# Cross attention tile loop: one stretch of projections, the value products between the two rounds of scores, and more buffers

## The reference

```python
qh = (q @ Wq.T).reshape(B, Lq, H, D).transpose(0, 2, 1, 3)
kh = (k @ Wk.T).reshape(B, Lk, H, D).transpose(0, 2, 1, 3)
vh = (v @ Wv.T).reshape(B, Lk, H, D).transpose(0, 2, 1, 3)
qh = _layernorm(qh, gq, bq) * scale
kh = _layernorm(kh, gk, bk)
attn = jax.nn.sigmoid(jnp.einsum('bhqd,bhkd->bhqk', qh, kh))
x = jnp.einsum('bhqk,bhkd->bhqd', attn, vh)
x = x.transpose(0, 2, 1, 3).reshape(B, Lq, C)
return x @ Wp.T + bp
```

## Time and profile before

| What | Value |
|---|---|
| Time, median of 3 runs | 3021.32 us (3021.06 to 3024.84) |
| The profiled execution's own time | 3023.51 us |
| Its span in the profile | 3021.8 us |
| Mean granted TensorE clock | 0.990 |
| PE busy | 2954.1 us, 98% of the span |
| ACT, DVE, POOL busy | 1474.4, 1409.8 and 873.7 us |

### The profile page before, as it was taken

How to read it: one execution, slowest core, us unless ns; L and a number is a source line. 1 busy time by engine, 2 the same in 40 slices (tenths; PEclk the granted TensorE clock), 3 DMA queues, 4 the chain that set the end, 5 groups by cost and what they waited for, 6 DMA issues and landing times.

```text
span 3021.8 us, 69076 instructions
## 1 busy us (share of the span) xinstructions
PE 2954.1 (98%) x28514; PEld 2327.0 (77%) x28514; DVE 1409.8 (47%) x1962; ACT 1474.4 (49%) x1450; POOL 873.7 (29%) x615
## 2 busy tenths in 40 slices
PE   6999999999999999999999999986999999999999
PEld 4777777777777777777777777753999998999998
DVE  5333333333333333333333333336658856657754
ACT  1444444444444444444444444440646555646554
POOL 3444444444444444444444444430000000000000
PEclk8999999999999999999999999997999999999999
DMA  5000000000000000000000010001455555555553
GB/s 202 28 24 28 24 28 24 28 24 28 24 28 24 28 24 28 24 28 24 28 24 28 24 28 24 28 1 56 154 181 182 183 194 195 195 183 190 178 188 133
DMA packets 53359, 231.64 MB, mean 77 GB/s; under 512 B 6056, under 2 KB 6312, under 8 KB 31920
## 3 DMA queue, kind: packets, MB, share of 16 engines
q1 hardware_dynamic: 53296, 230.74, 22.5%
HBM read 230.19 MB, written 0.52 MB: 76 GB/s over the span
## 4 chain that ended last, share of the span: by engine, by line
PE 95%; DVE 3%; issue 1%; ACT 1%; DMA 0%; POOL 0%; POOLq 0%; SPq 0%; DVEq 0%; ACTq 0%
PE kv_ps L1041 38%; PE f_ps L1288 22%; PE o_ps L1087 12%; PE s_ps L1075 12%; PE y_ps L1272 5%; PE kv_ps L1062 3%; PE pm L1155 1%; DVE w_lo L632 1%; DVE pre L909 0%; ACT w_hi L522 0%; PE pm L1203 0%; DMA wk_rows<-wk_dram 0%; PE kv_ps L1034 0%; PE pm L1144 0%; DVE lin_norm L809 0%
## 5 line engine op out<-in xcount | busy, mean ns | idle before, releaser
L483 ACT ACTIVATE probs<-s_ps 128x2048 f32<-128x2048 f32 x392 | 737.7, 1882 | 718.6 <-PE s_ps L1075 718.5
L429 POOL TENSOR_TENSOR k_var<-k_var,neg_half 128x16 f32<-128x16 f32 x196 | 571.0, 2913 | 15.5 <-POOL k_var L425 0.2
L419 POOL TENSOR_TENSOR ctx_lo<-ctx_raw,ctx_hi 128x512 fp32r<-128x512 f32 x196 | 251.8, 1285 | 1117.9 <-DVE ctx_hi L673 1117.9
L698 DVE TENSOR_TENSOR k_n<-k_centred,k_var 128x496 f32<-128x496 f32 x196 | 134.4, 686 | 711.4 <-POOL k_var L429 711.4
L632 DVE TENSOR_TENSOR w_lo<-w_raw,w_hi 128x2048 fp32r<-128x2048 f32 x160 | 366.4, 2291 | 175.4 <-ACT w_hi L522 175.3
L1288 PE MATMUL f_ps<-h_hi,w_hi 128*128 128x256 f32 x1536 | 428.8, 279 | 0.0
L1288 PE MATMUL f_ps<-h_lo,w_hi 128*128 128x256 f32 x1536 | 427.8, 279 | 0.0
L1288 PE MATMUL f_ps<-h_hi,w_lo 128*128 128x256 f32 x1536 | 427.8, 279 | 0.0
L1087 PE MATMUL o_ps<-probs,v_sb 128*32 128x256 f32 x6272 | 380.8, 383 | 0.2 <-ACT probs L483 0.2
L1041 PE MATMUL kv_ps<-wk_hi,ctx_hi 128*128 128x512 f32 x784 | 347.3, 443 | 4.3 <-DVE q_lo L751 2.8
L522 ACT ACTIVATE w_hi<-w_raw 128x2048 fp32r<-128x2048 f32 x160 | 305.9, 1913 | 70.2 <-PE y_ps L1272 62.4
(11 more groups left out here) (194 smaller groups left out, 4850.7 us busy)
## 6 DMA issues: line engine op xcount, KB each, us to landing
w_raw<-w_dram SPq DMA_DIRECT2D x160, 1024.0 KB, 4.8
ctx_raw<-ctx_dram SPq DMA_DIRECT2D x196, 256.0 KB, 2.6
qkv_w<-qkv_w_dram SPq DMA_DIRECT2D x1, 3072.0 KB, 13.1
bias_rows<-bias_rows_dram SPq DMA_DIRECT2D x1, 1280.0 KB, 16.6
wq<-wq_dram SPq DMA_DIRECT2D x1, 1024.0 KB, 5.5
wk_rows<-wk_dram SPq DMA_DIRECT2D x1, 1024.0 KB, 7.5
wv<-wv_dram SPq DMA_DIRECT2D x1, 1024.0 KB, 9.7
out_w<-out_w_dram SPq DMA_DIRECT2D x1, 1024.0 KB, 17.7
```

Of the source, the lines that this page charges most:

```text
L419: g.tensor_tensor(ctx_lo[r % 2][:], raw[r % 4][:], ctx_hi[r % 2][:].bitcast(f32), ALU.subtract).then_inc(ctx_lo_made, 1)
L429: g.tensor_tensor(k_var[:, 2], k_var[:, 1], neg_half[:].to_broadcast([P, H]), ALU.pow)\
L483: s.activation(probs[half][:], s_ps[:], ACT.Sigmoid).then_inc(probs_made, 1)
L698: v.tensor_tensor(k_n[:, :, 0:D - 1], k_c[:, :, 0:D - 1], per_row(k_var[:, 2], D - 1), ALU.mult)\
```

## The change

There are four buffers `v_sb` instead of two, and three `probs` instead of two: round 0 takes `probs[0]` and `probs[1]` by turns, round 1 always `probs[2]`. On PE a step now has the transposes of tile r-1 first, then all 24 projection matmuls of tile r, round 0 of tile r-1, the value products of tile r-2, and round 1 of tile r-1. On DVE the values of tile r are copied in step r, ahead of `normalise`, no longer in step r+1. ACT's round 0 no longer waits for the value products that stand ahead of it. Nothing after the attention is changed.

```diff
-        v_sb = [sb(f"v_sb{i}", [P, C], f32, attn) for i in range(2)]
-        probs = [sb(f"probs{i}", [P, HG, 2, TOK], f32, attn) for i in range(2)]
+        v_sb = [sb(f"v_sb{i}", [P, C], f32, attn) for i in range(4)]
+        probs = [sb(f"probs{i}", [P, HG, 2, TOK], f32, attn) for i in range(3)]
...
+        def probs_of(r, half):
+
+            return probs[2] if half else probs[r % 2]
...
                 act.wait_ge(s_made, n_of(it, r, 2, half + 1))
-                act.wait_ge(av_made, n_of(it, r, 2, half + 1))
-                s.activation(probs[half][:], s_ps[:], ACT.Sigmoid).then_inc(probs_made, 1)
+                wait(act, av_made, n_of(it, r, 2, 2 if half else -1))
+                s.activation(probs_of(r, half)[:], s_ps[:], ACT.Sigmoid).then_inc(probs_made, 1)
...
                 dve.wait_ge(v_made, n_of(it, r, 1, 1))
-                wait(dve, av_made, n_of(it, r, 2))
-                v.tensor_copy(v_sb[r % 2][:], kv_ps[:, 1]).then_inc(v_copied, 1)
+                wait(dve, av_made, n_of(it, r, 2, -4))
+                v.tensor_copy(v_sb[r % 4][:], kv_ps[:, 1]).then_inc(v_copied, 1)
...
-                copy_values(it, r - 1)
                 split_turned(it, r - 1)
                 if more:
                     high_part(it, r + 1)
                 if keys:
                     sum_squares(it, r)
+                    copy_values(it, r)
                     normalise(it, r)
...
+            copy_values(0, 0)
             normalise(0, 0)
...
-                if project_it:
-                    projection(it, r, 0, 6)
                 turn_keys(it, r - 1)
                 if project_it:
-                    projection(it, r, 6, 12)
+                    projection(it, r, 0, 24)
+                scores(it, r - 1, 0)
                 if not too_early(it, r - 2):
                     attend(it, r - 2, 0)
                     attend(it, r - 2, 1)
-                scores(it, r - 1, 0)
-                if project_it:
-                    projection(it, r, 12, 24)
                 scores(it, r - 1, 1)
```

More of the change, by code:

```diff
@@ L1086, in attend @@
                         first = P * grp + D * h
-                        ins = t.matmul(o_ps[D * h:D * h + D, grp], v_sb[r % 2][:, first:first + D],
-                                       probs[half][:, h, j], start=False, stop=False, skip_group_check=True)
+                        ins = t.matmul(o_ps[D * h:D * h + D, grp], v_sb[r % 4][:, first:first + D],
+                                       probs_of(r, half)[:, h, j], start=False, stop=False, skip_group_check=True)
                 ins.then_inc(av_made, 1)
             def step(it, r, project_it=True):
-                if project_it:
-                    projection(it, r, 0, 6)
                 turn_keys(it, r - 1)
                 if project_it:
-                    projection(it, r, 6, 12)
+                    projection(it, r, 0, 24)
+                scores(it, r - 1, 0)
                 if not too_early(it, r - 2):
```

## The result

The changed kernel takes 3001.15 us in the median of 4 runs (2998.84 to 3003.03); the kernel before takes 3023.03 us beside it (3021.06 to 3024.84). The ratio is 0.9927, 95% interval 0.991 to 0.9945: faster by 0.7%, 22 us. The profiled execution took 3001.42 us, its span is 2999.7 us, 22.1 less than before.

The account below looks back on a forecast made before the run. PE's back-to-back instructions were taken to bound the tile loop. The step would go from 10.07 to 10.05 us: 194 steps x -0.02 = -4, plus 1.5 one-time, gives -2.5 and 3019 us, range 3004 to 3032.

Parts of the forecast that it names:

- What bounds the kernel: Tile loop: PE never waits, so a step lasts as long as PE's instructions one behind the other, 10.07 us.
- Projections as one run of 24: PE's projections in a step: three runs (6, 6, 12) become one that settles to closer spacing, 5.34 us.
- The second rival: Second half of the 24 projections: the run does not settle, 0.07 us more per step, 3032 us; chance 0.10.
- Round 1 to transposes: PE from round 1 of scores to the transposes: 0.91 us, plus 0.06 between bounds of nothing and 0.10.
- Between the rounds: PE from round 0 to round 1: the sigmoid's 2.35 us outlasts the products' 2.11, a new wait of about 0.24.
- ACT's wait in one step of four: Sigmoid of round 0: its wait on a register instruction costs 0.08 to 0.09 us there, 0.02 per step.
- DVE's order: Values copied ahead of `normalise` on DVE: costs nothing, with 0.8 us left before the transposes would wait.
- The third rival: Transposes wait because DVE's copy stretches POOL's power: +114 us, 3135 us; chance 0.03.
- One-time: Outside the repeated steps: 2.6 us more at the start, 1.1 back at the end, together 1.5 more.
- Only the change-overs count: PE's step: fewer changes of matmul form, no wait for the sigmoid; step 9.81 us, total 2972 us; chance 0.05.
- The fourth rival: PE's clock falls because of a short idle piece in each step: +190 us if one step in ten, 3210; chance 0.02.
- The mechanism's own range: Forecast's wait of 0.24 us eating the saved change-over, chance 0.75: 2997 to 3036 us, mostly 3007 to 3028.

Follow-up runs that it names:

- e8: Changed kernel with PE's order of before, keeping only buffers, ACT's relaxed waits and DVE's earlier copy: 3027.36 us, ratio 1.0005 to the kernel before.
- e5: Changed kernel with PE's wait for the sigmoid on an event instruction ahead of the weight load in every loop step: 3024.78 us, ratio 0.9989.
- e2: Changed kernel with the sigmoid's two waits in the other order, so its wait for the scores stands on the sigmoid itself: 2996.5 us, ratio 0.9913.
- e3: Changed kernel with the value products ahead of round 0 instead of between the rounds: 3626.33 us in one run.
- e1: Changed kernel with PE's two waits of a scores round in the other order, which altered only the steps written out: 2998.23 us, ratio 0.9916.
- e6: Changed kernel with two `probs` buffers instead of three and ACT's waits on the value products as before: 3212.94 us in one run.

## Why the prediction was wrong, point by point

- **What bounds the kernel:** right. PE's instructions one behind the other set the step before; with PE's order alone restored (e8) the step is 10.073 again.
- **Projections as one run of 24:** right, 5.33 against 5.34. The run settles in the loop as in the first tile, and its wait at the first V matmul does not disturb it. The second rival falls. (Its run should have been 5.45, twice 2.84 less one distance of 0.23, and not 5.41.)
- **Round 1 to transposes:** right. 0.91, and the transposes then take 0.41 to the projections instead of 0.35; I had added 0.06 between bounds of 0 and 0.10.
- **Between the rounds:** the mechanism was right and its size off, and this is the step that failed. "The longer one ends last: 2.35, of which about 0.24 is a new wait of PE in every step" is 2.27 with a wait of 0.18. The figure came from the last tile, where the sigmoid's wait is on an event instruction ahead of the weight load; in the loop it is on the load itself. In unrounded starts it is 0.094 per step, and times 194 that is 18 of the 20 us by which the sum of -2.5 fell short of -22. The rest is rounding of the other terms, such as 5.34 for 5.33. In e5, where the loop has the event form, the step is the forecast's 10.05.
- **ACT's wait in one step of four:** right, 0.08 longer there, gone in e2 when the wait moved.
- **DVE's order:** right that nothing waits in the loop. `k_n` ends at 1007.56 and the transposes start at 1008.69, 1.1 later, where I had 0.8 left. The third rival did not come.
- **One-time:** 2.8 - 1.1 = 1.7 against 2.6 - 1.1 = 1.5, in part by luck. Of the 2.8, 0.8 is a setup that ran later, which the forecast had not; and the last transposes gave back 0.7, while the other 0.4 is what a last tile 1.0 longer and an untouched rest 1.5 shorter leave.
- **Only the change-overs count** (first rival, 9.81): not so in this kernel, since the wait for the sigmoid is there, at 0.18 a step. Without that wait the step would be 9.77, near the rival's 9.81.
- **The clock:** 1.00 as forecast. The fourth rival is real, at a longer idle piece (e3).

The mechanism's own range went down to 2997 (2995.5 by its own terms, since 1.5 was added twice), by a cheaper change from scores to transposes, a hidden register wait and a run of 5.30. None of these came so: all three stood near the forecast. I had put no bound on the 0.14 from the end of the sigmoid to PE, though a shorter way from one engine to another was in the rows: in the loop before, DVE's `k_n` starts 0.09 after POOL's power ends (1026.03 to 1026.12).

## What to carry to other kernels

A latency between engines that is read in one place holds for another only if the instruction waits there in the same way: look whether the late semaphore is on the instruction that does the work or on one ahead of it, and write the wait that is over last so that it lands on the working instruction. Where one buffer makes two engines take turns, compare the length of the covering work with that of the other engine's turn, from start to start: here the value products leave 0.18 of the sigmoid uncovered, and the fewer changes of form and longer runs are worth more than that. Whether another piece of work would cover it better was not tried. Before a stretch of matmuls is joined, list who else writes its bank, since a wait that was covered by what stood between comes out.

## What the runs showed of the hardware

- No weight load on PE carries two waits; the second stands on an event instruction (which can carry two, as in e5) or on a register instruction ahead of it. If the wait on the event is the one that is over last, the weight load starts 0.11 behind the releasing engine's end instead of 0.05, and the first matmul 0.14 instead of 0.05: in 3 steps of the changed kernel, in none with e1, and in all 196 with e5.
- A wait on a register instruction ahead of an ACT instruction costs 0.08 (0.396 instead of 0.318 from the last scores to the sigmoid in one step of four, 0.318 in all four with e2).
- The granted clock stayed at 1.00 with idle pieces of 0.18 and of 1.19 us in each step (of 9.95 and 11.01, the changed kernel and e6), and was 0.89 with 1.98 us in each step of about 13 (e3); there the projections were 0.43 instead of 0.23 apart for part of the step.
- A run of like projections settles from 0.23 to 0.227 apart within some ten of them, in the loop as in the setup.
